# A fused decoder layer: row statistics of x1 and x2 from accumulated sums and ScalarE squares, and another order of stage two

## The reference, cut to what matters

```python
x = x + linear_attention(layernorm(x))      # 8 heads, feature map elu+1            -> x1
x = x + cross_attention(layernorm(x), ctx)  # 77 keys; each row of scores is normalised
                                            # (mean, std), masked, softmaxed        -> x2
x = x + moe(layernorm(x))                   # 8 experts, top 2, capacity 1280, GELU -> out
# layernorm: (x - mean) / sqrt(var + 1e-5), no scale or shift
```

## Time and profile before

| what | before |
|---|---|
| median of 3 runs | 1626.31 us (1625.48 to 1629.68) |
| the profiled execution: its time, its span | 1626.16 us, 1624.5 us |
| mean granted TensorE clock | 0.954 |
| busy PE, DVE, ACT, POOL over the span | 1469.5, 673.6, 525.0, 360.0 us |
| busy PE, DVE, ACT, POOL in 400.8 to 429.6 us (one body of stage two) | 23.08, 25.11, 12.40, 16.29 us |

### The profile page before, as it was taken

The page is one execution under the profiler, slowest core; times in us unless marked ns, Lnnn a source line. Parts: engine busy times, 40 slices in busy tenths (PEclk is TensorE's granted clock), DMA queues, the critical chain, the costliest instruction groups (busy, mean ns, idle before and its releaser), DMA issues.

```text
span 1624.5 us, 20795 instructions
## 1 busy us (share of the span) xinstructions
PE 1469.5 (90%) x7326; PEld 1229.4 (76%) x7327; DVE 673.6 (41%) x1423; ACT 525.0 (32%) x849; POOL 360.0 (22%) x354
## 2 busy tenths in 40 slices
PE   6999999988776199999979999997999999997998
PEld 4877877767665077888968878896888888896886
DVE  6634656578888324312242431213531431213311
ACT  4333434243524124322322432214522432223311
POOL 3211223145645401120211212021112022021011
PEclk9999999999986599999999999998999999999999
DMA  9200222144335624320252352025442242024022
GB/s 189 53 1 26 84 99 68 37 130 156 98 105 130 188 65 138 84 39 6 47 156 54 81 150 52 0 52 143 136 123 52 65 132 50 0 52 143 8 43 26
DMA packets 79019, 132.47 MB, mean 82 GB/s; under 512 B 30388, under 2 KB 30516, under 8 KB 77912
## 3 DMA queue, kind: packets, MB, share of 16 engines
q1 hardware_dynamic: 62520, 97.40, 20.4%
q0 software_dynamic: 16416, 34.16, 11.3%
HBM read 93.63 MB, written 37.91 MB: 81 GB/s over the span
## 4 chain that ended last, share of the span: by engine, by line
PE 80%; DVE 7%; issue 4%; DMA 4%; ACT 3%; POOL 2%; ACTq 0%; SPq 0%; POOLq 0%; DVEq 0%
PE pg L877 15%; PE pg L878 14%; PE pg L879 14%; PE pj L877 8%; PE pj L879 8%; PE pj L878 8%; PE pg L1132 2%; PE pj L1105 2%; DMA stage<-w 2%; PE pg L1070 1%; PE pt L1227 1%; DVE w_lo L1290 1%; POOL slot_table L577 1%; PE pt L895 1%; DMA out_rows<-ost,etab 1%
## 5 line engine op out<-in xcount | busy, mean ns | idle before, releaser
L877 PE MATMUL pg<-xe_hi,w_hi 128*128 128x512 f32 (+2 forms) x1088 | 397.0, 365 | 44.8 <-DVE hp L1667 23.8
L878 PE MATMUL pg<-xe_lo,w_hi 128*128 128x512 f32 (+2 forms) x1088 | 395.0, 363 | 0.0
L879 PE MATMUL pg<-xe_hi,w_lo 128*128 128x512 f32 (+2 forms) x1088 | 394.4, 363 | 0.0
L1667 DVE TENSOR_TENSOR hp<-gl,pg 128x512 f32<-128x512 f32 (+1 forms) x136 | 86.9, 641 | 634.0 <-ACT gl L830 623.4
L637 POOL DMA_INDIRECT out_rows<-ost,etab x62 | 99.8, 1610 | 829.0 <-ACT ost L857 392.4
L877 PEld LDWEIGHTS pg<-xe_hi,w_hi 128*128 128x128 f32 x1088 | 209.2, 192 | 78.0 <-DVE hp L1667 25.4
L879 PEld LDWEIGHTS pg<-xe_hi,w_lo 128*128 128x128 f32 x1088 | 209.0, 192 | 28.7
L878 PEld LDWEIGHTS pg<-xe_lo,w_hi 128*128 128x128 f32 x1088 | 209.3, 192 | 28.3
L830 ACT ACTIVATE gl<-pg 128x512 f32<-128x512 f32 (+1 forms) x136 | 75.9, 560 | 433.6 <-PE pg L879 429.9
L877 PE MATMUL pj<-w_hi,hg_hi 128*128 128x512 f32 x464 | 183.5, 395 | 0.0
L879 PE MATMUL pj<-w_hi,hg_lo 128*128 128x512 f32 x464 | 181.0, 390 | 0.0
(11 more groups left out here) (229 smaller groups left out, 1957.5 us busy)
## 6 DMA issues: line engine op xcount, KB each, us to landing
stage<-w SPq DMA_DIRECT2D x96, 512.0 KB
xr<-x SPq DMA_DIRECT2D x8, 1024.0 KB, 8.9
out_rows<-xr SPq DMA_DIRECT2D x8, 1024.0 KB, 4.5
x_rows<-xn SPq DMA_DIRECT2D x8, 1024.0 KB
x_in<-x SPq DMA_DIRECT2D x7, 1024.0 KB, 5.4
late_xT<-xT_hi SPq DMA_DIRECT2D x2, 1024.0 KB, 3.9
late_xT<-xT_lo SPq DMA_DIRECT2D x2, 1024.0 KB, 6.0
xT_hi<-late_xT SPq DMA_DIRECT2D x2, 1024.0 KB
```

The source lines that it names most:

```text
L877: nc.tensor.matmul(o, lh, rh, start=start, stop=False)
L878: nc.tensor.matmul(o, lh, rl, start=False, stop=False)
L879: return nc.tensor.matmul(o, ll, rh, start=False, stop=stop)
L1667: v.tensor_tensor(hp[j % 2][:, 0:w], gl[j % 2][:, 0:w], pg[:, 2 + j % 2, 0:w], ALU.mult).then_inc(s_hp, 1)
```

## The change

The statistics of x1 and x2 are no longer taken by `bn_stats` and `bn_aggr` on DVE. The instruction that adds the residual also writes the sum of each row (`accum_out`), a small DVE instruction makes the negative mean, and ACT takes the sum of the squares of (x minus mean) with one `Square` activation per tile that also writes its sum. POOL makes 1/std from that. The bias of the softmax is the mean of the scores, which `bn_aggr` has anyway, in place of the maximum. The second pair of the attention output is done before `logits` and `route`. `positions` uses bank `pj[1]` and comes after `values`; every third late job (place 2) uses `pj[0]`, and places 1 and 2 both stand at the end of PE's body, after `attend(g + 2)`. ACT does the late jobs of place 1 after the exponentials of the scores.

```diff
-LATE_AT = {(-1, 0): [0], (-1, 2): [1], (0, 0): [2], (0, 1): [3], (0, 2): [4], (1, 0): [5], (1, 1): [6],
+LATE_AT = {(-1, 0): [0], (-1, 1): [1], (0, 0): [2], (0, 1): [3], (0, 2): [4], (1, 0): [5], (1, 1): [6],
            (1, 2): [7], (2, 0): [8], (2, 1): [9], (2, 2): [10], (3, 0): [11], (3, 1): [12], (3, 2): [13],
            (4, 0): [14], (4, 1): [15]}
+BANK = {s: 0 if place == 2 else 1 for (g, place), jobs in LATE_AT.items() for s in jobs}
...
+def late_until(g, place):
+    return sum(len(jobs) for at, jobs in LATE_AT.items() if at <= (g, place))
...
+            def inverse_std_of(q, squares):
+                step(p.tensor_scalar(var_e[q][:], squares[:], 1.0 / D, LN_EPS, ALU.mult, ALU.add))
+                return p.tensor_tensor(rstd[q][:], var_e[q][:], half_neg[:], ALU.pow)
...
             def rstd_1(g):
-                pool.wait_ge(s_stat1, g + 1)
-                inverse_std(0).then_inc(s_rstd1, 1)
+                pool.wait_ge(s_sq, max(8 * g, TI))
+                inverse_std_of(0, sq1).then_inc(s_rstd1, 1)
...
             def norm3(g):
-                pool.wait_ge(s_stat3, g + 1)
+                pool.wait_ge(s_sq, min(8 * g + 12, 8 * GROUPS))
                 if g:
                     pool.wait_ge(s_xn3, g * TI)
-                p.tensor_scalar(neg_mean[1][:], mv[1][:, :, 0], -1.0, None, ALU.mult)
-                step(inverse_std(1))
-                p.tensor_tensor(shift[1][:], neg_mean[1][:], rstd[1][:], ALU.mult).then_inc(s_rstd3, 1)
+                step(inverse_std_of(1, sq3))
+                p.tensor_tensor(shift[1][:], neg3[:], rstd[1][:], ALU.mult).then_inc(s_rstd3, 1)
...
+            def squares(g, pair, means, negative, to):
+                act.wait_ge(means, 2 * g + pair + 1)
+                for i in range(2 * pair, 2 * pair + 2):
+                    if made[0] >= TI:
+                        act.wait_ge(s_sq, made[0] - TI + 1)
+                    a.activation(junk[i][:], xr[g % 4][:, i, :], ACT.Square, bias=negative[:, i:i + 1],
+                                 accum_out=to[:, i:i + 1]).then_inc(s_sq, 1)
+                    made[0] += 1
...
-            turned_rows(xT2, range(TI), 1)
+            for pair in range(2):
+                squares_1(0, pair)
+                turned_rows(xT2, range(2 * pair, 2 * pair + 2), 1)
...
             score_exp(0)
+            late_q(late(-1, 1))
             for g in range(GROUPS):
                 turned(sT[:], 0)
                 late_q(late(g - 1, 2))
                 if g >= 1:
                     normalise3(g - 1)
                 if g + 1 < GROUPS:
+                    squares_1(g + 1, 0)
                     turned_rows(xT2, range(2), 1)
                     late_q(late(g, 0))
+                    squares_1(g + 1, 1)
+                    turned_rows(xT2, range(2, TI), 1)
+                squares_3(g)
+                if g == GROUPS - 2:
+                    for s in range(4):
+                        split(0, s)
+                gate_exp(g)
+                if g + 1 < GROUPS:
+                    score_exp(g + 1)
                     late_q(late(g, 1))
-                    turned_rows(xT2, range(2, TI), 1)
-                    if g == GROUPS - 2:
-                        for s in range(4):
-                            split(0, s)
-                    gate_exp(g)
-                    score_exp(g + 1)
-            gate_exp(GROUPS - 1)
             normalise3(GROUPS - 1)
...
                     if s == 0:
                         pe.wait_ge(s_feat, JA)
+                    elif place == 2:
+                        pe.wait_ge(s_sev, g + 2)
                     else:
-                        pe.wait_ge(s_qfree, s)
+                        pe.wait_ge(s_qfree, s if late(g, 2) == [] or place else late_until(g - 1, 1))
+                    if place == 1 and g >= 0:
+                        pe.wait_ge(s_posev, g + 1)
...
             def sums(g, at):
                 pe.wait_ge(s_btev, at)
+                pe.wait_ge(s_qfree, late_until(g - 1, 2))
...
             def positions(g):
                 pe.wait_ge(s_hot, g + 1)
+                pe.wait_ge(s_qfree, late_until(g, 0))
...
             for g in range(GROUPS):
                 more_groups = g + 1 < GROUPS
                 at_e = turn_exp(g)
                 if more_groups:
                     attend(g + 1, range(2, TI))
                 sums(g, at_e)
-                late_q(late(g, 0))
                 if more_groups:
                     at_x1 = turn_x1(g + 1, range(2))
-                    late_q(late(g, 1))
-                    positions(g)
+                late_q(g, 0)
                 values(g, range(2))
                 if more_groups:
                     at_x1.update(turn_x1(g + 1, range(2, TI)))
                 values(g, range(2, TI))
+                positions(g)
                 if more_groups:
                     scores(g + 1, at_x1)
                     if g + 2 < GROUPS:
                         attend(g + 2, range(2))
-                    late_q(late(g, 2))
-                else:
-                    positions(g)
+                    late_q(g, 1)
+                    late_q(g, 2)
...
                 for q in range(2):
                     i = 2 * pair + q
-                    v.tensor_tensor(x1[:, i, :], x1[:, i, :], kf[q][:], ALU.add).then_inc(s_x1, 1)
+                    v.scalar_tensor_tensor(x1[:, i, :], kf[q][:], 1.0, x1[:, i, :], ALU.mult, ALU.add,
+                                           accum_out=sum1[:, i:i + 1]).then_inc(s_x1, 1)
                 dve.wait_ge(s_x1, g * TI + 2 * pair + 2)
-                ins = stats(x1, 0, range(2 * pair, 2 * pair + 2))
-                if pair == 1:
-                    link(ins)
-                    aggregate(0, s_stat1)
+                two = slice(2 * pair, 2 * pair + 2)
+                v.tensor_scalar(neg1[:, two], sum1[:, two], -1.0 / D, None, ALU.mult).then_inc(s_neg1, 1)
...
-                v.tensor_reduce(smax[:], sc[:], AX.X, ALU.max)
...
-                v.scalar_tensor_tensor(nbias[:], smax[:], -1.0, sig[:, 3], ALU.mult, ALU.mult).then_inc(s_ex, 1)
+                v.scalar_tensor_tensor(nbias[:], mv2[:, :, 0], -1.0, sig[:, 3], ALU.mult, ALU.mult).then_inc(s_ex, 1)
...
             def cross_out(g):
-                for i in range(TI + 1):
-                    m = g * TI + i
-                    if i < TI:
-                        dve.wait_ge(s_x2p, m + 1)
-                        v.scalar_tensor_tensor(x2[:, i, :], pg[:, i, :], sinv[:, i:i + 1], x2[:, i, :],
-                                               ALU.mult, ALU.add).then_inc(s_x2t, 1)
-                    if i >= 1:
-                        dve.wait_ge(s_x2t, m)
-                        ins = v.bn_stats(st[1][:, i - 1, :], x2[:, i - 1, :])
-                link(ins)
-                aggregate(1, s_stat3)
+                for i in range(TI):
+                    dve.wait_ge(s_x2p, g * TI + i + 1)
+                    v.scalar_tensor_tensor(x2[:, i, :], pg[:, i, :], sinv[:, i:i + 1], x2[:, i, :],
+                                           ALU.mult, ALU.add, accum_out=sum3[:, i:i + 1]).then_inc(s_x2t, 1)
+                    if i % 2:
+                        two = slice(i - 1, i + 1)
+                        dve.wait_ge(s_x2t, g * TI + i + 1)
+                        v.tensor_scalar(neg3[:, two], sum3[:, two], -1.0 / D, None, ALU.mult).then_inc(s_neg3, 1)
...
                     for s in range(2):
                         split(0, s)
+                if more_groups:
+                    attention_out(g + 1, 1)
                 logits(g)
                 route(g)
-                if more_groups:
-                    attention_out(g + 1, 1)
-                    positions_out(g)
                 cross_out(g)
+                positions_out(g)
                 if more_groups:
                     score_stats(g + 1)
-                else:
-                    positions_out(g)
                 slots(g)
```

More of the change, by code:

```diff
@@ L123, in decoder @@
     zz = keep("zz", [P, 2, 2, 4])
-    smax = keep("smax", [P, TI])
+    sum1, neg1, sq1, sum3, neg3, sq3 = (keep(n, [P, TI]) for n in ("sum1", "neg1", "sq1", "sum3", "neg3", "sq3"))
     nbias = keep("nbias", [P, TI])
@@ L208, in decoder @@
     xT2 = alias("xT2", [P, KC, GT], F32, one_at + 8192 * 6)
+    junk = [alias(f"junk{i}", [P, D], F32, one_at + 8192 * 7 + 2048 * i) for i in range(TI)]
     wk_raw = alias("wk_raw", [P, KC, D], F32, one_at + 8192 * 6)
@@ L309, in decoder @@
         s_x1 = sem("x1_tile_ready")
-        s_stat1 = sem("x1_stats_ready")
+        s_neg1 = sem("x1_means_ready")
+        s_sq = sem("rows_squares_summed")
         s_rstd1 = sem("x1_rstd_ready")
@@ L747, in late_q, with squares_1, squares_3 @@
                     i, c = s % 2, slice(s % KC, s % KC + 1)
-                    a.activation(fe[i][:], pj[1][:], ACT.Relu, bias=bq_neg[:, c], scale=-1.0
+                    o = pj[BANK[s]]
+                    a.activation(fe[i][:], o[:], ACT.Relu, bias=bq_neg[:, c], scale=-1.0
```

(28 more changed lines are left out.)

11 lines of the change are left out of this document (5 added, 6 removed).

## The result

| | before | after |
|---|---|---|
| median (lowest to highest, runs) | 1627.89 us (1625.48 to 1629.68, 4) | 1556.57 us (1553.74 to 1561.16, 4) |
| ratio, with its 95% interval | | 0.9566 (0.9537 to 0.9594) |
| profiled execution: span | 1624.5 us | 1554.0 us |
| mean granted clock | 0.954 | 0.969 |

Faster, as forecast, but by 71 us where 30.4 stood in the forecast, and outside the range. The two spans differ by 70.5 us, and I first asked in which stage. I cut both traces at the same four places: T of group 0, T of group 7, the first matmul of the experts, the end.

The account below looks back on a forecast made before the run. No engine filled a middle stretch of stage two; PE waited at three places. Stretch gains 3.9 + 6.7 + 5.0 + 4.5 + 5.0 + 4.6 + 2.0, less 1.3 before the loop: 1626.2 - 30.4 = 1595.8 us, range 1588 to 1612.

Parts of the forecast that it names:

- The floor of PE: Stage two, stretches with three late jobs: PE's own work, 23.3 us with gaps between unlike shapes, is the least time.
- the 1.0 us for handovers that miss each other: Middle stretches of stage two: PE's and ACT's close loops miss each other now and then; 24.3 us taken per stretch.
- The wait of 3.8: Stage two, ACT's wait from squares of x2 through norm3, sigma and softmax: 1.8 + 1.4 + 0.6 us.
- ACT's loop of 22.6: Middle stretches of stage two: ACT's 18.8 us of work plus its 3.8 wait, close to PE's 23.3.
- the `kf` wait: Stage two, g = 6: PE's values waits for the second attention output pair; 2.9 us at most, 2.0 taken as gain.
- The 0.6 of allowance: Stretch g = 0: added to PE's 20.5 us and 1.2 for exponentials covered by one job, giving 22.3.
- Before the loop: Ahead of stage two's loop: squares delay the copies for PE's second transposes, 3.2 less 1.9 of cover, loss 1.3 us.
- ACT paces: Rival, chance 0.20: squares at 1.18 us make ACT's loop set stage two's pace, 26.6 us with misses; gain 18, 1608.
- A doubled DVE instruction: Rival, chance 0.06: the sum doubles DVE's two-input x1 additions, 2.1 us per group, 0.8 a stretch; 1601.
- Another table: Rival, chance 0.04: Square needs another activation table than Exp, four loads or 5.1 us per group on ACT; 1619.
- Slower softmax: Rival, chance 0.04: softmax gets behind the squares at 1.99 us each, 4 us more in six stretches; 1650.
- Gain taken back: Rival, chance 0.06: two or three handovers come later than assumed, PE idle as before; 1626.

Follow-up runs that it names:

- squares_twice: The changed kernel with every square on ACT done a second time into a buffer that nothing reads: 1578.20 us, 0.9710 of before.
- pair_after_route: The changed kernel with the second pair of the attention output back behind logits and route on DVE: 1571.03 us, 0.9652 of before.
- old_order: The kernel before with only the new statistics (sums, squares on ACT, mean as softmax bias), order and banks as they were: 1602.74 us, 0.9835 of before.

## Why the prediction was right in direction and wrong in size

**Stage three, 28.6 us: the step that failed.** The sum was made over stage two alone, and the prediction took stage three as unchanged; it named "stage three of another length" only as a sign of being wrong. The runs show that the instructions added on ACT moved its expert loop from place 437 to 595, out of a stall of some 7 us per turn. Shown by padding in both directions. It has nothing to do with what these instructions compute. Why 53 stalls and 61 doesn't (modulo 128) was not settled. The rows for it stood open before: 63.0 us of idle "issue" ahead of eight table loads on ACT.

**The middle stretches, g = 1 to 4: 26.4 against 21.2.** The floor of PE was right in kind: 22.57 busy of 22.70, where 23.3 was taken. Mis-sized were that floor, by 0.7, and the 1.0 us for handovers that miss each other: they didn't, but for 1.2 us in g = 2. The exponentials start at T + 4.26 in g = 2 (361.65 and 365.91), forecast 4.4; DVE came to 18.8 (20.3) and ACT to 17.7 (18.8). The wait of 3.8 from the squares of x2 through `norm3`, `sigma` and softmax was sized about right (3.6 in `squares_twice`), but in the changed kernel it is not on the path: the squares end 0.7 us before T, and the exponentials go by the statistics of the scores, so ACT's loop of 22.6 was no second limit beside PE's.

**g = 5 and g = 6: 6.7 and 6.4 against 4.6 and 2.0.** Here the failed step is the clock. The prediction took g = 6 "with a cold clock" as before, so only the `kf` wait could go. Nor was the 2.9 of the earlier trace rows all a wait for `kf`: PE waited 1.7 us for `hot` there, since `positions` stood ahead of `values`, and 0.66 for `kf`. In g = 6 the waits that went are under 2 us; PE's busy time fell from 21.38 to 16.04 us for the same 114 matmuls. `pair_after_route` shows the chain: a wait of 3.1 us returns in g = 5, the granted clock in g = 6 is 0.70 in place of 0.92, and PE's own work there takes 5.2 us more. Here a wait ahead of PE cost more than its length. How far the other waits, those for `sc`, hold the clock down was not settled.

**g = 0: 5.0 against 3.9.** The 0.6 of allowance and some of the 1.2 were not needed.

**Before the loop: -3.45 against -1.3.** The wait was sized right: it grew from 1.58 to 2.98 us, 1.4, and the scores behind it ran without a gap, so the cover was there. What the sum left out is the clock. From the second transposes to the end of the scores it was 0.73, where it had been 1.00; the transposes took 1.48 us against 1.12 and the scores 5.02 against 3.71, 1.7 us together. Another 0.4 came in before the first transposes, which start at 307.33 and not 306.91.

**The end, +0.8 against 0**: as forecast within the spread of that part.

Added up: 44.5 - 3.45 + 0.8 + 28.6 = 70.5.

**The rivals.** *ACT paces*: no, a square takes 0.71 us of ACT with what shows of its read, forecast 0.80; `squares_twice` bounds it. *A doubled DVE instruction*: no. The undisturbed `scalar_tensor_tensor` with two inputs and a sum takes 0.69, as without a sum; its mean is 0.81 because some lie beside POOL (one of them, 1.75 us, beside a POOL addition of 1.62). The rule of the Trainium skill on DVE cited in the prediction is not borne out here. *Another table*: no, Square and Exp ran on one load. *Slower softmax*: no. *Gain taken back*: no. All of them were ways to gain less. The low end of the range, 1588, allowed 6.8 us more than the forecast, from PE's floor, g = 5 and g = 0 alone, and nothing outside stage two.

## What to carry to other kernels

Idle "issue" time ahead of the same instruction in every turn of a loop, with packets on that engine's instruction queue, is worth a test before anything else: a few fulfilled waits ahead of the loop move its place and cost nothing that shows, and here they took 27 us out of stage three, of 1627 in all. Pad the two kernels to the same kind of place before comparing an edit that changes an engine's instruction count, or take the stages apart, or `old_order` looks like a gain that it isn't. And when PE waits at two handovers while DVE is nearly full, relieve DVE and move the filler work together: in stage two the order alone gained 28 us and the statistics alone nothing, both together 44.5.

## What was unexpected of the hardware

The place of ACT's loop in its program matters: 8 to 9 us of idle time ahead of the table load of a turn against 1 to 2, 28.6 us of stage three over seven turns. Eight instructions ahead of the loop were enough to remove it (place 445 against 437). The eight places tried fit a period of 128 instructions, and also one of 64, but a period of 256 does not fit. A sum beside the result costs 0.197 us on ACT, of which 0.10 shows, and 0.08 on DVE. In the last two stretches, where PE had waited for `sc`, `hot` and `kf`, the granted clock was 0.76 and 0.69; in the changed kernel, with 1.32 and 4.05 us of waits for `sc` and 0.97 and 0.35 for `kf` left, it was 0.92, and with the pair of the attention output put back 0.87 and 0.70.
